# Scan slot re-divided: lane halves on GpSimd, four-lane mix on VectorE, experts' gates on ScalarE, weight splits spread out

## The reference

```python
def _combine(left, right, W):            # LANES = 4, hd = 32
    q = left.reshape(B, T, LANES, hd)
    k = right.reshape(B, T, LANES, hd)
    v = ((left + right) @ W).reshape(B, T, LANES, hd)
    scores = jnp.einsum('btld,btmd->btlm', q, k) * hd ** (-0.5)
    att = jax.nn.softmax(scores, axis=-1)
    z = jnp.einsum('btlm,btmd->btld', att, v)
    denom = (1.0 + jnp.arange(LANES, dtype=z.dtype))[None, None, :, None]
    z = _rms_norm(z) / denom
    return left + z.reshape(B, T, C)

def _pscan2(x, W, identity):             # 9 levels: d = 1, 2, ..., 256
    d = 1
    while d < T:
        ident = jnp.broadcast_to(identity.astype(x.dtype), (B, d, C))
        shifted = jnp.concatenate([ident, x[:, :-d]], axis=1)
        x = _combine(shifted, x, W)
        d *= 2
    return x

def _L1_ffn_ref(x, gate_w, gate_b, w1, b1, w2, b2):     # 8 experts, top 2
    ...
    h = jax.nn.relu(jnp.einsum('nd,edh->neh', x_flat, w1) + b1)
    y = jnp.einsum('neh,eho->neo', h, w2) + b2
    out_flat = jnp.einsum('ne,neo->no', dense_gate, y)

x = L0_attn_x
...                                       # layer 0
xn = _layernorm(x, axis=-1)
s = _L1_attn_ref(xn, ...)                 # scan, times xn @ W_v.T, projected
g = _silu(_L1_ffn_ref(xn, ...))
x = x + s * g
```

## Time and profile before

| | |
|---|---|
| median of 3 runs | 639.1 us (638.64 to 639.62) |
| profiled execution | 638.24 us, of which the span of the profile is 636.5 us |
| busy: PE, DVE, ACT, POOL | 532.1, 525.6, 261.9, 397.3 us |
| mean granted TensorE clock | 0.945 of full |
| chain that ended last | DVE 40%, PE 31%, issue 17%, ACT 5%, POOL 5% |

### The profile page before, as it was taken

The page is one execution under the profiler, slowest core; times in us unless marked ns, Lnnn a source line. Parts: engine busy times, 40 slices in busy tenths (PEclk is TensorE's granted clock), DMA queues, the critical chain, the costliest instruction groups (busy, mean ns, idle before and its releaser), DMA issues.

```text
span 636.5 us, 8860 instructions
## 1 busy us (share of the span) xinstructions
PE 532.1 (84%) x2918; PEld 410.6 (65%) x2918; DVE 525.6 (83%) x993; ACT 261.9 (41%) x607; POOL 397.3 (62%) x367
## 2 busy tenths in 40 slices
PE   4979999999999992759888888888888888886855
PEld 3746666665666661748676776776776776775635
DVE  7576857856865664498999999999999999999875
ACT  3332332252252242035446446445455455454232
POOL 6920011032032059537999999999999999999954
PEclk9999999999999996597999999999999999999676
DMA  8330000000000000100111111101101111101002
GB/s 249 119 132 2 1 1 1 1 2 16 0 2 17 1 0 17 34 0 18 34 33 34 35 33 33 50 18 51 34 18 50 34 33 34 34 18 33 18 1 66
DMA packets 16598, 20.79 MB, mean 33 GB/s; under 512 B 2344, under 2 KB 10160, under 8 KB 16428
## 3 DMA queue, kind: packets, MB, share of 16 engines
q1 hardware_dynamic: 16556, 20.26, 10.5%
HBM read 9.76 MB, written 1.05 MB: 17 GB/s over the span
## 4 chain that ended last, share of the span: by engine, by line
DVE 40%; PE 31%; issue 17%; ACT 5%; POOL 5%; DMA 0%; DVEq 0%; ACTq 0%; POOLq 0%
PE bank L569 30%; DVE shared L1437 9%; DVE bank L1449 9%; DVE shared L1443 7%; ACT shared L1094 3%; DVE shared L1472 2%; PE bank L572 2%; POOL wgu_lo L462 1%; DVE shared L1457 1%; DVE ssum L1467 1%; ACT shared L1092 1%; DVE shared L1302 1%; DVE smax L1453 1%; DVE shared L1307 1%; POOL wgu_hi L460 1%
## 5 line engine op out<-in xcount | busy, mean ns | idle before, releaser
L569 PE MATMUL bank<-xnT_lo,wgu_hi 128*128 128x512 f32 x264 | 121.1, 459 | 8.7 <-ACT shared L1106 6.9
L569 PE MATMUL bank<-w,shared 128*128 128x128 f32 x1024 | 121.1, 277 | 0.0
L569 PEld LDWEIGHTS bank<-w,shared 128*128 128x128 f32 x1024 | 118.4, 194 | 0.2 <-ACT shared L1106 0.2
L569 PE MATMUL bank<-xnT_hi,wgu_lo 128*128 128x512 f32 x264 | 105.7, 400 | 0.0
L569 PE MATMUL bank<-xnT_hi,wgu_hi 128*128 128x512 f32 x264 | 105.3, 399 | 0.0
L512 POOL TENSOR_TENSOR shared<-shared 128x1024 f32<-128x1024 f32 x36 | 85.1, 2365 | 27.3 <-DVE shared L1472 27.3
L569 PE MATMUL bank<-shared 128*128 128x512 f32 (+3 forms) x280 | 89.4, 440 | 1.9 <-ACT shared L953 1.2
L1449 DVE TENSOR_REDUCE bank<-shared 128x64 f32<-128x2048 f32 x36 | 82.6, 2295 | 3.9 <-POOL shared L494 2.7
L1106 ACT ACTIVATE shared<-bank,b_now 128x512 f32<-128x512 f32 x128 | 80.6, 682 | 0.3
L975 ACT ACTIVATE shared<-bank 128x512 f32<-128x512 f32 x68 | 40.6, 598 | 94.1 <-PE bank L569 91.0
L1302 DVE TENSOR_TENSOR shared<-shared,bank 128x512 f32<-128x512 f32 x64 | 43.8, 685 | 40.5 <-PE bank L569 30.1
(11 more groups left out here) (180 smaller groups left out, 880.7 us busy)
## 6 DMA issues: line engine op xcount, KB each, us to landing
w<-in_w SPq DMA_DIRECT2D x8, 256.0 KB, 3.1
shared<-in_w SPq DMA_DIRECT2D x1, 2048.0 KB, 9.2
left_tok<-state_ext SPq DMA_DIRECT2D x16, 128.0 KB
left_tok<-state_ext SPq DMA_DIRECT2D x8, 192.0 KB
shared<-in_wd SPq DMA_DIRECT2D x1, 1088.0 KB, 11.7
x<-in_x SPq DMA_DIRECT2D x4, 256.0 KB, 3.9
out<-x SPq DMA_DIRECT2D x4, 256.0 KB, 2.3
left_tok<-state_ext SPq DMA_DIRECT2D x4, 254.0 KB
```

The costliest lines, as they stand in the source:

```text
L569: return nc.tensor.matmul(out, lhsT, rhs, start=start, stop=stop)
```

## The change

Six edits:

1. `add_lanes` (two halves into z) moves from VectorE to GpSimd, right behind `halve_mix`.
2. The fourth lane: VectorE's mix takes all four lanes in one operation, straight from PSUM, and waits for `v_mm` and `sexp_done`; GpSimd's `last_mix` and ScalarE's copy of the fourth lane go. The score products take all four lanes on VectorE in odd slots; GpSimd's `last_product` stays for even slots.
3. Gate times expert result goes to ScalarE (`gated`, four operations a block, in place in PSUM, for expert 0 into `acc`); VectorE adds the block in one 512-wide operation (none for expert 0). PE's waits on `ffn_acc` are changed to suit.
4. VectorE's order in a slot: the expert sum in one piece behind the shift, and `square_sum` at the slot's end, behind the mix. Its loop over levels is written out.
5. The copies of biases and gates (`b1_now`, `gate1_now`) go.
6. GpSimd's splits of w1 are spread over the last batch; `acc` is not cleared, and of `ecmp` only the diagonal is.

```diff
-            for b in range(B):
+            for b in range(B - 1):
                 state_product(b)
...
                 attention_tokens(b)
+            state_product(B - 1)
+            token_rest1(B - 3)
+            pool.wait_ge(s("ld_w1"), 16)
+            split_expert(0)
+            add_to_x(B - 2)
+            for e in range(1, 6):
+                split_expert(e)
+            normalise1(B - 2)
+            attention_tokens(B - 1)
+            split_expert(6)
             token_rest1(B - 2)
-            pool.wait_ge(s("ld_w1"), 16)
-            pool.wait_ge(s("u_mm"), item((B - 1) * PAIRS) + 1)
-            for e in range(E1):
-                split_expert(e)
+            split_expert(7)
...
-            g.memset(ecmp[:], 0.0).then_inc(s("ecmp_zero"), 1)
-            g.memset(acc[:], 0.0).then_inc(s("acc_zero"), 1)
+            g.memset(ecmp[:].rearrange("p t a b -> p t (a b)")[:, :, 0:E1 * E1:E1 + 1], 0.0).then_inc(s("ecmp_zero"), 1)
...
+            def add_lanes(k, b):
+                pool.wait_ge(s("mix2_done"), k + 1)
+                m = mix2[:, b % 2].rearrange("p j l m d -> p (j l) m d")
+                g.tensor_tensor(z[:, b % 2].rearrange("p j (l d) -> p (j l) d", l=LANES), m[:, :, 0], m[:, :, 1],
+                                ALU.add).then_inc(s("z_done"), 1)
...
                 if before:
                     halve_mix(k - 1, (b - 1) % B)
+                    add_lanes(k - 1, (b - 1) % B)
...
                 if ahead:
                     sum_inputs(k + 1, (b + 1) % B)
-                    last_product(k + 1, (b + 1) % B)
-                if this:
-                    last_mix(k, b)
+                    if b % 2 == 1:
+                        last_product(k + 1, (b + 1) % B)
...
-                    after(pe, s("ffn_acc"), n * TB)
+
+                    after(pe, s("ffn_gated"), n * TB)
+                    after(pe, s("ffn_acc"), n - B)
...
+            def gated(e, blk):
+
+                n = e * B + blk
+                act.wait_ge(s("gate1_done"), 1)
+                act.wait_ge(s("ffn_down"), n + 1)
+                for j in range(TB):
+                    t, y = blk * TB + j, bank[7][:, j * P:(j + 1) * P]
+                    a.activation(acc[:, t] if e == 0 else y, y, ACT.Copy, scale=gate1[:, t, e:e + 1]).then_inc(s("ffn_gated"), 1)
...
                 if then:
                     then()
+                if down:
+                    gated(*down)
                 if up:
...
             def products(k, b):
 
+                lanes = LANES - 1 if b % 2 == 0 else LANES
...
             def scores(k, b):
                 dve.wait_ge(s("prod_done"), k + 1)
-                dve.wait_ge(s("last_prod"), k + 1)
+                if b % 2 == 0:
+                    dve.wait_ge(s("last_prod"), k // 2 + 1)
...
+                dve.wait_ge(s("v_mm"), k + 1)
+                dve.wait_ge(s("sexp_done"), k + 1)
+                values = bank[2][:].rearrange("p (j m d) -> p j m d", j=TB, m=LANES).unsqueeze(2)
+                tt(mix[:, b % 2], sexp[:, b % 2].unsqueeze(4).broadcast_to([P, TB, LANES, LANES, LD]),
+                   values.broadcast_to([P, TB, LANES, LANES, LD]), ALU.mult).then_inc(s("mix_done"), 1)
+
+            def expert_sum(e, blk):
+
+                n = e * B + blk
+                if e > 0:
+                    dve.wait_ge(s("ffn_gated"), TB * (n + 1))
+                    part = acc[:, blk * TB:(blk + 1) * TB].rearrange("p j c -> p (j c)")
+                    tt(part, part, bank[7][:], ALU.add).then_inc(s("ffn_acc"), 1)
...
                 if this:
                     products(k, b)
-                if this:
                     scores(k, b)
-                if before:
-                    add_lanes(*prev)
-                if summed:
-                    expert_gates(*summed)
-                if this:
                     score_max(k, b)
-                if summed:
-                    expert_sum(*summed, range(0, 1))
-                if this:
                     softmax_shift(k, b)
                 if summed:
-                    expert_sum(*summed, range(1, TB))
+                    expert_sum(*summed)
+                if this:
+                    exp_sum(k, b)
+                    mix_values(k, b)
                 if before:
                     square_sum(*prev)
-                if this:
-                    exp_sum(k, b)
-                if this:
-                    mix_values(k, b)
```

More of the change, by code:

```diff
@@ L830, in values @@
                 pe.wait_ge(s("sumT_cp"), k + 1)
-                after(pe, s("v_cp"), k)
                 after(pe, s("mix_done"), k)
@@ L1080, in left_out @@
                 a.copy(bank[1][:], left_tok[:, b].rearrange("p j c -> p (j c)")).then_inc(s("left_tok_cp"), 1)
-            def values_out(k, b):
-                act.wait_ge(s("v_mm"), k + 1)
-                a.copy(v_last[:, b % 2], bank[2][:].rearrange("p (j c) -> p j c", j=TB)[:, :, (LANES - 1) * LD:]).then_inc(s("v_cp"), 1)
             def expo(k, b):
@@ L1105, in relu, with slot @@
                 after(act, s("ffn_down"), e * B + blk)
-                a.activation(hT[:, c], bank[UP[c]][:], ACT.Relu, bias=b1_now[:, c:c + 1]).then_inc(s("ffn_relu"), 1)
-            def slot(k, b, this=True, before=True, ahead=True, up=None, then=None):
-                if this:
-                    values_out(k, b)
+                a.activation(hT[:, c], bank[UP[c]][:], ACT.Relu, bias=b1[:, e, c:c + 1]).then_inc(s("ffn_relu"), 1)
+            def gated(e, blk):
[5 more added lines that the diff above has]
+                    a.activation(acc[:, t] if e == 0 else y, y, ACT.Copy, scale=gate1[:, t, e:e + 1]).then_inc(s("ffn_gated"), 1)
+            def slot(k, b, this=True, before=True, ahead=True, up=None, down=None, then=None):
                 if ahead:
@@ L1132, in slot @@
                     relu(*up, 3)
-                    if up[1] == 0:
-                        act.wait_ge(s("gate1_done"), 1)
-                        after(act, s("ffn_acc"), up[0] * (B * TB))
-                        a.copy(gate1_now[:], gate1[:, :, bass.ds(up[0], 1)].rearrange("p t e -> p (t e)")).then_inc(s("gate_now_done"), 1)
             def level(lev, last=False):
@@ L1140, in level @@
                     up = (lev, j + 1) if j < B - 1 else None if last else (lev + 1, 0)
-                    slot(lev * B + (j + 1), (j + 1) % B, up=up)
+                    slot(lev * B + (j + 1), (j + 1) % B, up=up, down=(lev, j))
             act.wait_ge(s("x1_done"), B)
@@ L1516, in _ @@
             dve.wait_ge(s("gate1_done"), 1)
-            dve.wait_ge(s("acc_zero"), 1)
-            with dve.Fori(0, LEVELS - 1) as lev:
+            for lev in range(LEVELS - 1):
                 for j in range(B):
@@ L1523, in _ @@
                 if k == 2:
-                    dve.wait_ge(s("ffn_acc"), E1 * B * TB)
+                    dve.wait_ge(s("ffn_acc"), (E1 - 1) * B)
                     for b in range(B):
```

51 lines of the change are left out of this document (8 added, 43 removed).

## The result

The changed kernel takes 696.2 us (median of four runs, 693.0 to 698.6) against 639.4 for the one before: 1.089 times as long, 95% interval 1.083 to 1.094. The forecast was 658 us, with a range up to 669. So the sign was right and the size was not: of the 57 us it lacks 38.

A forecast was written before the change was run, and what follows sets the result against it. VectorE bounds the kernel at 9.62 us a slot; the change makes a ring of 10.77. Slot 6 at 318.5, 27 slots of 290.8, then 29.0, 17.8 and 1.74 give 658 us, range 644 to 669.

The forecast's parts named there:

- The wait and its place: VectorE's 512-wide addition waits for ScalarE's gated products, holding up the slot's tail; VectorE idles some 2.4 us a slot.
- The ring's length: From one mix's end to the next, through sum of squares, relus, matmuls, gated products and addition: 10.77 us, +1.15 a slot.
- Rival 1: ScalarE's gated products cost as a bare copy: slot 10.37 us, kernel 646 us; chance 0.12.
- TensorE's clock: Forecast kept it full inside the scan; a rival had it fall there, 695 us or more, chance 0.05.
- The price at the lower clock: The block of 32 matmuls on TensorE takes 5.12 us at the lower clock for 3.74.
- the rival's 1.38: Least growth per slot, in us, if TensorE's clock falls inside the scan: 695 us or more; chance 0.05.
- Rival 2: The wait costs nothing and VectorE stays the bound at 8.27 us a slot: 586.6 us; chance 0.06.
- The start: Before the scan, spread splits let GpSimd's first sums start 7.1 us sooner, near 249.5; slot 1's products start at 273.3.
- Rival 4: The splits of w1 do not shorten the start, being late where they now stand: 664.5 us; chance 0.07.
- Slots 1 to 5 and the tail: Slot 6 starts at 318.5, 9.7 us ahead of before; the tail after the last mix takes 17.8 us for 16.71.
- From slot 33 to the last mix: Stretch held by TensorE at its lower clock: 29.0 us instead of 31.96.
- GpSimd: Even with nothing lost, at most 10.15 us a slot, under 10.77, so its shifted work costs nothing; its addition takes 1.27.

The follow-up runs named there:

- the fill: Changed kernel, with the last group of the experts' first matmuls in each slot computed three times into the same bank: 666.1 us, ratio 1.042 to the kernel before.

## Why the prediction was wrong, point by point

- **The wait and its place: right.** VectorE idles in front of the 512-wide sum, released by the gated products, with the tail of the slot queued behind it. The runs show it as the cause: with the sum behind the mix, and nothing else changed, 696 becomes 604 us.
- **The ring's length: right.** 10.90 at full clock for 10.77 forecast, in every slot once the clock is kept up by the fill. Rival 1 (products at the price of a bare copy) is out: 0.34 us each and 1.11 for four, near the relu's row and not the copy's 0.78 for four.
- **TensorE's clock: the step that failed.** The sum held no term for the clock, and the runs put 37.8 us in its place. The prediction saw the longer pause, even put a size on it (2.3 us; it is 2.67), priced what follows ("the ring would grow by at least 1.38 a slot: 658 + 37 = 695 or more"), and then set it aside: "with its present pauses the clock stays full for 260 us, and 8.4 us of 10.8 remain work". Neither half of this argument bore on the case. The row showed a full clock under two short pauses a slot; the change makes a single long one out of them, and about that the row says nothing. TensorE's waits between 330 and 540 us (engine and line, waited for: us in total, times, longest), before:

```profile
PE bank L569 <- DVE shared L1472: 17.7, 21, 0.9
PE bank L572 <- POOL shared L488: 13.8, 22, 0.7
```

  and after:

```profile
PE bank L569 <- ACT shared L1075: 45.4, 17, 2.7
```

  So it was 1.5 us a slot in two pieces, and is 2.7 in one. The slot of 10.77 was the sum with TensorE at 2.4 GHz only, so a term that depends on the forecast's own outcome was taken from the state before. The low-clock row was at hand, the 5.12 of the earlier trace rows, and in front of it in the trace of the kernel before stands a pause that could have been read as a warning. Here are two pauses (the number in square brackets) in front of groups of matmuls, then the windows around them, with the granted clock as the third number from the end:

```profile
274.21 0.50 PE L569 MATMUL bank<-xnT_lo,wgu_hi 128*128 128x512 f32 x1 [3.24 <-ACT shared L1106]
...
286.49 0.79 PE L569 MATMUL bank<-xnT_lo,wgu_hi 128*128 128x512 f32 x1 [3.70 <-ACT shared L1106]
```

```profile
270.00:286.40 16.40, 9.47 (x62) 7.52 (x60) 15.79 (x34) 5.69 (x15) 6.01 (x4) 1.00 0.00 0
286.49:290.37 3.88, 3.48 (x11) 2.69 (x12) 3.85 (x5) 2.48 (x6) 1.90 (x1) 0.50 0.00 0
290.37:295.25 4.88, 4.88 (x34) 4.88 (x33) 3.80 (x3) 0.76 (x2) 4.72 (x6) 0.70 0.05 15
```

  Behind the pause of 3.70 us the clock was at 0.50; behind the one of 3.24 it stayed at 1.00. So the trace of before held a fall after a pause, but could not say where harm begins.
- **The price at the lower clock: about right, in part by luck.** The 5.12 of the earlier trace rows was read as the price of 32 matmuls at the lower clock. The stretch it fills had a mean clock of 0.70, so only part of it ran at the lower one. In the changed kernel too the lower clock covers only part of a slot: the 32 matmuls take 1.63 more in the slot shown (5.47 for 3.84), with 0.05 more elsewhere, nothing in the slots of 10.9, and the slots of 13.55 have 2.65 more. The mean of 1.40 a slot comes out near the rival's 1.38, which was meant for every slot.
- **Rival 2** (the wait costs nothing, 8.27 a slot) failed in the changed kernel, but it is nearly what moving the sum to the slot's very end brings: 8.72 a slot, the 8.27 of work plus a wait of 0.32 and small gaps.
- **The start: right.** The two waits beside the splits went as forecast. Slot 1 starts 1.3 us later than forecast, of which 1.2 were there long before the first split; in the run with the gates on VectorE and the squares in front it starts at 273.34, for 273.3 forecast. The splits alone, tested apart, gave 5.4. Rival 4 is out.
- **Slots 1 to 5 and the tail: right** to 0.2 us each. **From slot 33 to the last mix** it was 2.1 us less than forecast. The forecast has TensorE at its lower clock hold that stretch; in the changed kernel VectorE is busy for 25.34 of the 26.91 us, so it was hardly held by anything else. No run tests that stretch apart.
- **GpSimd: right.** It is busy 215.34 / 27 = 8.0 us a slot, and its additions take 1.26 to 1.32 us in the 27 slots, with VectorE's lane addition gone.

Between the profiled execution's span of 696.6 and the forecast one of 656.1 lie 40.5 us: 37.8 for the clock, 3.5 for a ring of 10.90 instead of 10.77, 1.3 for the start, less 2.1 from slot 33 on; the rest is under 0.2.

What the parts are worth, read from the medians: the splits -5.4; with lane additions, mix and last products re-divided too -18.5 (621.1 against 639.6); with the gates on ScalarE, the squares behind the mix and the expert sum behind everything -37.8 (601.8 against 639.6); with the same sum in front of the mix +57.

Open: what exactly decides when the clock falls. Among the kernels whose pause recurs in every slot, a longer single pause goes with a lower clock (last section); but no run changes the pause alone.

## What to carry to other kernels

Where work is handed to an engine with time to spare, the instruction that takes the result back holds up all that is queued behind it on the busy engine: put it as late as its result is needed, and add up the ring through both queues before and after. When a change lengthens the ring, ask what it does to TensorE's pauses, and price its matmuls at both clocks; a profile in which short pauses are harmless is no evidence on a long one. If the granted clock is under suspicion, let TensorE repeat a matmul in the pause: if that makes the kernel faster, the clock was a cause.

## What the runs showed of the hardware

One recurring pause of TensorE, in slots of about 10 to 11 us at full clock, went with these granted clocks between 330 and 540 us: 2.67 us, 0.86; 1.98, 0.94; 1.90, 0.98 (fell twice in 27 slots); 1.48, 1.00; 1.30, 1.00. Two pauses a slot of 1.51 and 0.43 or 0.95 went with 1.00 though TensorE was busy for only 165.92 us of the 210; with the gates on VectorE and one pause of 1.90 it was busy for 171.82, with as many matmuls (1155 against 1149), and its clock fell. So in this pair the kernel with the lower busy time kept its clock. Two kernels that differ in more than their pauses don't prove a rule, and no run here only splits a pause. Nor does the length of one pause tell all: the single pause of 3.24 us in the kernel before left the clock at 1.00, where pauses of 2.67 us in every slot did not.

The Trainium skill, "TensorE: Matmul & The Clock Gate", section "HAM oscillation — how this bites in real kernels", tells of a kernel in which the waits between tiles let the clock fall anew in every tile. These runs agree in kind: 22 of the 27 slots lost time to a clock that fell again and again. By that section's rule for idle gaps the pauses of 2.67 us here would have been harmless; the granted clock of 0.86 says otherwise, and the measurement decides.
